# Moving 34 columns in place of 136 in the attention's products with the values

## The chip, the cores and the metric

The kernel runs on one core of a Trainium2 chip. The metric is the device time in microseconds (us) of one execution. Three executions of the kernel before took 1523.86, 1524.19 and 1518.64 us; the median is 1523.86 us. A fourth execution was profiled and took 1523.76 us.

## The reference

The input x has 4 sequences of 1024 tokens with 256 channels. Three layers follow one another, each on a layer norm of x and each added to x:

- a gated delta-rule attention with 16 heads of 16, whose state runs over the tokens in order;
- a cross attention on a context of 64 tokens;
- a feed-forward layer: a causal convolution, a pointwise product, a mixture of 8 experts of which 2 are taken, a norm and a small gelu network.

The change touches the cross attention alone. Cut to what matters it is:

```
q = (query @ Wq.T)   as 32 half heads of 8;  k likewise;  v = (value @ Wv.T) as 16 heads of 16
q1, q2 = q[:, :16], q[:, 16:];  k1, k2 = k[:, :16], k[:, 16:]
a1 = softmax(q1 k1^T * 8**-0.5) @ v
a2 = softmax(q2 k2^T * 8**-0.5) @ v
attn = a1 - lam * a2            # then a norm per head, and attn @ Wp.T + bp
```

## The kernel before, in words

The tokens are worked in 8 tiles (NI) of 4 sequences by 128 tokens. A tile has a first half (the recurrent attention, with its chunk steps z, d1, cs and co, its projections and the 16-token blocks "raw") and a second half (the cross attention and the feed-forward layer). The code is unrolled. Work of several tiles is interleaved: while the recurrence of one tile runs, the second half of the tile before it runs too, and the projections of the next tiles. The order of each engine is written out by hand in the lists ORDER["pe"], ORDER["dve"], ORDER["act"] and ORDER["pool"]; the engines meet through semaphores. The table KEEP says where TensorE issues products of the identity with itself, `keep` (line 1532), into a bank that nobody reads. They are left out wherever bank 7 is in use for good, which is most of the loop: the profile has none of them between 228 and 1222 us.

The cross attention of a tile runs in 8 units u. A unit is one sequence and 8 of its 16 heads:

- `sc` (line 1821) computes the scores of the 8 heads, 32 contraction rows at a time, into banks 4 and 5.
- VectorE takes the maxima (L1306) and subtracts them (L1312); ScalarE exponentiates (L786).
- `pt` (line 1841) transposes the probabilities, four heads per call, and ScalarE copies them to SBUF (L794).
- `pv` (line 1856) is the step that changes. For each of the 8 heads the transposed probabilities (128 by 128: two half heads with 64 context tokens each) are the stationary operand, and rows of vx_sb the moving one. A head owns 34 columns of vx_sb: for each half head 16 values and a column that gives the sum of the probabilities. The product of head h is written to the bank from column 34 h on.
- VectorE then takes the reciprocal of the sums (L1323) and forms a1 - lam * a2 (L1329, L1331, L1333).

Before the change each product of `pv` moves 136 columns, those of its own head and of the three that follow, and writes 136 columns of the bank. The columns behind its own 34 are overwritten by the products of the next heads, or are not read after the last. So that the last heads have something to read, vx_sb is 102 columns longer, and these are set to zero at the start (line 904).

All operands of these products are 4-byte floats. The profile shows every such product as two LDWEIGHTS and two MATMUL records. A unit has 8 products, so it is a block of 16 records of each kind; there are 8 units in each of 8 tiles: 64 blocks, 1024 records.

In the last tile the second half runs alone, and the units alternate between two sets of banks and buffers (`values_bank`, `probT_of`).

Of the kernel before, what the change touches and what calls it, by code (L numbers as in the profile page):

```python
# [25 lines left out]
P = 128  # L26
B, S, D = 4, 1024, 256
H, DH = 16, 16
NK = 64
NE, HID = 8, 64  # L30
# [8 lines left out]
NP_ = B * G * NC  # L39
# [40 lines left out]
class Chain:  # L80
# [16 lines left out]
    def do(self, ins):  # L97
        self.link(ins)
        self.wait()
# [86 lines left out]
def build(nc, x, out, weights, consts, cols, scratch, biases):  # L186
    ctx = ExitStack()
    with ctx:
        def sb(name, shape, dt=F32):
            return ctx.enter_context(nc.sbuf_tensor(name, shape, dt))  # L190
# [46 lines left out]
        ones3 = sb("ones3", [P, P], BF16)  # L237

        kbx = sb("kbx", [P, 2, B, 4 * NK])
        vx_sb = sb("vx_sb", [P, (B * H + 3) * 34])  # L240
# [6 lines left out]
        zc = sb("zc", [P, B])  # L247
        state = sb("state", [P, 4, G * B, DH])
        decayed = sb("decayed", [P, 4, G * B, DH])
        halo = sb("halo", [P, 6, B, 3])  # L250
        fT = sb("fT", [P, KC, B, TB + 2])
# [13 lines left out]
        vT = sb("vT", [P, NC, D])  # L265
# [10 lines left out]
        M3 = sb("M3", [P, NP_ + 1, CH])  # L276
# [30 lines left out]
        def values_bank(j):  # L307

            return bank[2 if j == NI - 1 else 6]
# [5 lines left out]
        def probT_of(j, u):  # L315
            flat_ = last_probT if j == NI - 1 and u % 2 else cs[:, 4, :]
            return flat_.rearrange("p (h t) -> p h t", h=8)
# [24 lines left out]
        gT = cs[:, 7, T:2 * T]  # L342
# [552 lines left out]
        def _(dve):  # L895
# [4 lines left out]
            do(V.memset(eps5, 1e-5))  # L900
            do(V.memset(eps6, 1e-6))
            do(V.memset(bias3[:, :], 0.0))
            for t_, value in ((ones3[:, :], 1.0), (zc[:, :], 0.0), (state[:, :, :, :], 0.0), (vT[:, :, :], 0.0), (M3[:, NP_:, :], 0.0), (vx_sb[:, B * H * 34:], 0.0), (fT[:, :, :, 0:2], 0.0), (halo[:, :, :, :], 0.0), (gT[HID:P, :], 0.0), (gT[HID:HID + 1, :], 1.0)):
                do(V.memset(t_, value))

            dve.wait_ge(ld_l, 16)
# [569 lines left out]
        def _(pe):  # L1476
            mm = nc.tensor.matmul
# [317 lines left out]
            def second(j):  # L1795
                def up(name, k=1):
                    pe.wait_ge(ev[name].sem, ev[name].at(j, k))

                def fin(name, ins):
                    ins.then_inc(ev[name].sem, 1)  # L1800
# [43 lines left out]
                def pv(u, n):  # L1844
                    b, hc = u // 2, u % 2
                    up("pt_sb", 2 * u + n + 1)
                    if n == 0:
                        if j == NI - 1:
                            if u:
                                up("a_sb", u)  # L1850
                        else:
                            up("pt_sb", 2 * u + 2)
                    for h in range(4 * n, 4 * n + 4):

                        at = (b * H + 8 * hc + h) * 34
                        last = mm(values_bank(j)[:, 34 * h:34 * h + 136], probT_of(j, u)[:, h, :], vx_sb[:, at:at + 136], start=True, stop=True)  # L1856
                    if n:
                        fin("pv_ps", last)

# [91 lines left out]
                def ffu_(p):  # L1951
                    up("gelu", p + 1)
                    for n in range(2):
                        b = 2 * p + n
                        last = mm(bank[TAIL[p]][:, D * n:D * n + D], gT[:, b * TB:b * TB + TB], ffu, start=True, stop=True)
                    fin("ffu_ps", last)

                return {"turn2": turn2, "qx": qx_, "sc": sc, "pt": pt, "pv": pv, "turn3": turn3, "wp": wp_, "turn4": turn4, "pw": pw_, "router": router, "moe": moe,
                        "turn5": turn5, "mi": mi, "mo": mo, "turn6": turn6, "ffd": ffd_, "ffu": ffu_}

# [86 lines left out]
```

## Time and profile before

| what | value |
|---|---|
| median of the three runs | 1523.86 us |
| time of the profiled execution | 1523.76 us |
| its span, first to last instruction | 1522.0 us |
| TensorE (PE) busy | 1433.8 us, 94% |
| weight loads (PEld) busy | 954.3 us, 63% |
| VectorE (DVE) busy | 1171.5 us, 77% |
| ScalarE (ACT) busy | 829.3 us, 54% |
| GpSimd (POOL) busy | 203.4 us, 13% |
| mean granted TensorE clock | 0.993 of 2.4 GHz |
| line 1856, MATMUL | 1024 records of 128 x 136 |

Busy is the time in which an engine has at least one instruction in flight; overlapping instructions are counted once. The mean duration of one MATMUL record is therefore longer than the distance between two of them. PEld is the loading of stationary operands, which overlaps the products. The granted clock is 1.00 at 2.4 GHz and 0.50 at 1.2 GHz; a stretch with a value between the two has been at both levels.

### The profile page before, as it was taken

What the parts mean: (1) busy time and instruction counts of PE and PEld (TensorE: products, weight loads), DVE (VectorE), ACT (ScalarE), POOL (GpSimd) and SP (SyncE); (2) the same over time, 40 slices, a digit from 0 to 9 for tenths busy, and PEclk for the clock granted to TensorE, in tenths of its full rate; (3) what the DMA queues carried; (4) which work ended last, traced back from release to release, by engine and by line L of the source; (5) the groups of instructions that cost most, each with busy time, mean ns of one, the idle gap of its engine ahead of it and who ended that gap; (6) DMA issues with size and microseconds to landing.
All of it is one profiled execution on the core that took longest, in us unless ns stands there. A gap on an engine that the chain in (4) does not pass through costs nothing.

```text
span 1522.0 us, 38260 instructions
## 1 busy us (share of the span) xinstructions
PE 1433.8 (94%) x15839; PEld 954.3 (63%) x15870; DVE 1171.5 (77%) x3193; ACT 829.3 (54%) x1596; POOL 203.4 (13%) x212
## 2 busy tenths in 40 slices
PE   3988999999999999999999999999999988999998
PEld 1654666755766566755766566755766567756765
DVE  7457878977897878977797878877797778855753
ACT  2555365646665565645665565645665564534443
POOL 0121111102200121102200122102200022101000
PEclk9999999999999999999999999999999999999999
DMA  5010001000100001100100001000100001000000
GB/s 234 1 29 30 2 22 15 24 1 15 29 29 2 2 29 16 30 2 15 29 29 2 2 21 23 31 1 16 29 15 2 2 29 24 8 1 15 1 1 14
DMA packets 20213, 31.28 MB, mean 21 GB/s; under 512 B 1480, under 2 KB 17864, under 8 KB 19784
## 3 DMA queue, kind: packets, MB, share of 16 engines
q1 hardware_dynamic: 20040, 28.82, 6.5%
q8 instruction: 127, 2.08, 0.6%
q14 instruction: 46, 0.38, 0.1%
HBM read 20.41 MB, written 8.39 MB: 19 GB/s over the span
## 4 chain that ended last, share of the span: by engine, by line
PE 79%; DVE 13%; ACT 5%; issue 2%; POOL 0%; DVEq 0%; ACTq 0%
PE bank L1913 15%; PE bank L1856 7%; PE bank L1482 6%; PE bank L1612 6%; PE four L1703 4%; PE bank L1821 4%; PE bank L1841 4%; PE bank L1507 4%; PE four L1771 3%; PE bank L1615 3%; PE bank L1532 3%; PE four L1755 2%; PE four L1507 2%; PE bank L1514 2%; PE four L1722 2%
## 5 line engine op out<-in xcount | busy, mean ns | idle before, releaser
L1913 PE MATMUL bank<-w_sb,cs 128*128 128x512 f32 x512 | 246.9, 600 | 1.5 <-ACT cs L840 0.3
L551 POOL TENSOR_TENSOR decayed<-state,pk 128x512 f32<-128x512 f32 x64 | 68.1, 1064 | 848.2 <-DVE state L1222 848.2
L840 ACT ACTIVATE cs<-bank 128x512 f32<-128x512 f32 x128 | 76.3, 596 | 182.8 <-PE bank L1488 85.9
L1913 PEld LDWEIGHTS bank<-w_sb,cs 128*128 128x128 f32 x512 | 94.3, 190 | 88.5 <-issue 81.3
L1430 DVE SCALAR_TENSOR_TENSOR cs<-cs,rwt 128x256 f32<-128x256 f32 x224 | 98.7, 487 | 42.1 <-ACT cs L840 42.1
L1856 PEld LDWEIGHTS bank<-vx_sb,cs 128*128 128x128 f32 x896 | 108.4, 189 | 27.4 <-ACT cs L794 18.0
L1856 PE MATMUL bank<-vx_sb,cs 128*128 128x136 f32 x896 | 119.3, 284 | 5.1 <-ACT cs L794 3.1
L1612 PE MATMUL bank<-hT,w_sb 128*128 128x512 f32 (+1 forms) x224 | 107.5, 602 | 3.0 <-ACT hid L662 1.4
L794 ACT COPY cs<-bank 128x512 f32<-128x512 f32 x116 | 67.5, 582 | 74.5 <-PE bank L1841 73.8
L1081 DVE SCALAR_TENSOR_TENSOR qkv<-pre,l_sb,qkv 128x512 f32<-128x512 f32 x144 | 100.4, 746 | 0.0
L786 ACT ACTIVATE cs<-cs 128x1024 f32<-128x1024 f32 x60 | 63.4, 1056 | 56.3 <-DVE cs L1312 55.8
L1306 DVE TENSOR_REDUCE pkc<-bank 128x8 f32<-128x512 f32 x120 | 77.6, 683 | 18.9 <-PE bank L1821 16.7
L1312 DVE TENSOR_TENSOR cs<-bank,pkc 128x512 f32<-128x512 f32 x120 | 77.0, 683 | 14.5 <-PE bank L1841 14.1
L1841 PE MATMUL bank<-c_sb,cs 128*128 128x128 f32 x464 | 74.1, 282 | 10.7 <-ACT cs L794 5.6
L586 ACT ACT_TABLE_LOAD x64 | 82.1, 1283 | 1.1
L1821 PE MATMUL bank<-kbx,cs 32*128 32x256 f32 x480 | 79.2, 400 | 1.4 <-ACT cs L781 1.4
L1482 PE MATMUL bank<-cs,w_sb 128*128 128x256 f32 (+1 forms) x320 | 79.8, 389 | 0.6 <-issue 0.2
L1205 DVE SCALAR_TENSOR_TENSOR shared<-four,c_sb 128x256 f32<-128x256 f32 x128 | 55.9, 478 | 23.8 <-PE four L1722 22.8
L1841 PEld LDWEIGHTS bank<-c_sb,cs 128*128 128x128 f32 x464 | 49.7, 140 | 36.5 <-issue 24.1
L1703 PEld LDWEIGHTS four<-kq,shared 64*64 64x64 f32 x2048 | 63.9, 135 | 13.3 <-issue 13.2
L1532 PEld LDWEIGHTS bank<-c_sb 128*128 128x128 f32 x550 | 68.0, 199 | 6.2 <-issue 5.4
L1703 PE MATMUL four<-kq,shared 64*64 64x48 f32 x2048 | 69.6, 220 | 2.2 <-POOL shared L533 1.1
(257 smaller groups left out, 2994.6 us busy)
## 6 DMA issues: line engine op xcount, KB each, us to landing
xt<-in_x SPq DMA_DIRECT2D x8, 512.0 KB, 4.9
vscr<-qkv SPq DMA_DIRECT2D x8, 512.0 KB, 2.7
vT<-vscr SPq DMA_DIRECT2D x32, 128.0 KB, 4.4
Tm<-in_x SPq DMA_DIRECT2D x8, 512.0 KB, 3.9
out<-cs SPq DMA_DIRECT2D x8, 512.0 KB, 2.9
w_sb<-in_weights SPq DMA_DIRECT2D x1, 3656.0 KB, 18.5
w_sb<-in_weights SPq DMA_DIRECT2D x1, 1456.0 KB, 8.5
cs<-in_scratch SPq DMA_DIRECT2D x3, 256.0 KB, 8.8
```

The lines of the kernel that those rows point to most:

```text
L586: nc.scalar.preload_act_table_set(name)
L1081: ins = stt(dst, pre[:, n % 4, :, t:TB + t], L("conv", 4 * n + t, 4 * n + t + 1), dst, ALU.mult, ALU.add)
L1430: ins = stt(comb[:, b, :], src, wgt, comb[:, b, :], ALU.mult, ALU.add)
L1482: last = mm(dst, lhs(k), rhs(k), start=k == 0, stop=k == n - 1)
L1507: last = mm(dst[:, D * n:D * n + D], lhs[:, k, b * TB:b * TB + TB], rhs[:, k, :], start=False, stop=n == 1 and k == 1)
L1532: mm(bank[7 if i > 0 else 6][:, 0:P], ident, ident, start=True, stop=True)
L1612: mm(dst, ctrl[:, k, at:at + n], hT[:, k, :], start=k == 0, stop=False)
L1703: last = mm(bank[RAW[c % 4]][q, 48 * n:48 * n + 48], kqb[q, c % 2, n, :], kq[q, g, b, c, :, :].rearrange("p x t -> p (x t)"), start=True, ...
L1821: last = mm(scores(j, u, a)[:, 256 * f:256 * f + 256], qx[r:r + 32, f, b * TB:b * TB + TB], kbx[r:r + 32, f, b, :], start=True, stop=True)
L1841: last = nc.tensor.transpose(turned_bank(j, n)[:, h * P:h * P + P], prob[:, 4 * n + h, :], ident)
L1856: last = mm(values_bank(j)[:, 34 * h:34 * h + 136], probT_of(j, u)[:, h, :], vx_sb[:, at:at + 136], start=True, stop=True)
L1913: mm(dst, x1T[:, k, b * TB:b * TB + TB], ew[:, k, ep * 512:ep * 512 + 512], start=k == 0, stop=False)
```

## The change

Each product of `pv` moves and writes the 34 columns of its own head. The zeroing of the 102 further columns of vx_sb is dropped, as nothing reads them any more. The buffer keeps its size; order, semaphores, banks and the KEEP table stay.

```diff
-            for t_, value in (... (M3[:, NP_:, :], 0.0), (vx_sb[:, B * H * 34:], 0.0), (fT[:, :, :, 0:2], 0.0), ...):
+            for t_, value in (... (M3[:, NP_:, :], 0.0), (fT[:, :, :, 0:2], 0.0), ...):
                 do(V.memset(t_, value))
...
                     for h in range(4 * n, 4 * n + 4):
                         at = (b * H + 8 * hc + h) * 34
-                        last = mm(values_bank(j)[:, 34 * h:34 * h + 136], probT_of(j, u)[:, h, :], vx_sb[:, at:at + 136], start=True, stop=True)
+                        last = mm(values_bank(j)[:, 34 * h:34 * h + 34], probT_of(j, u)[:, h, :], vx_sb[:, at:at + 34], start=True, stop=True)
```

## Rows read from the trace of the kernel before

**Rows 1.** The page: span; busy us, share, instructions; granted clock in 40 slices.

```profile
span 1522.0 us, 38260 instructions
PE 1433.8 (94%) x15839; PEld 954.3 (63%) x15870; DVE 1171.5 (77%) x3193; ACT 829.3 (54%) x1596; POOL 203.4 (13%) x212
PEclk9999999999999999999999999999999999999999
```

**Rows 2.** The page: the chain that ended last, by engine.

```profile
PE 79%; DVE 13%; ACT 5%; issue 2%; POOL 0%; DVEq 0%; ACTq 0%
```

**Rows 3.** Groups by line and shape: busy us, mean ns of one, idle before.

```profile
L1856 PE MATMUL bank<-vx_sb,cs 128*128 128x136 f32 x896 | 119.3, 284 | 5.1 <-ACT cs L794 3.1
...
L1897 PE MATMUL bank<-w_sb,cs 128*128 128x8 f32 x128 | 16.5, 252 | 1.3 <-DVE cs L1380 1.3
```

**Rows 4.** Windows, line 1856 alone: stretch, length, busy (records), clock, DMA.

```profile
228.00:1222.00 994.00, 102.27 (x768) 1.00 0.06 16
1222.00:1315.00 93.00, 17.06 (x128) 1.00 0.09 24
1394.00:1456.00 62.00, 16.86 (x128) 1.00 0.03 10
```

**Rows 5.** Timeline, one block of line 1856: start us, length us, what.

```profile
745.26 1.92 PEld L1856 LDWEIGHTS bank<-vx_sb,cs 128*128 128x128 f32 x16
745.26 2.12 PE L1856 MATMUL bank<-vx_sb,cs 128*128 128x136 f32 x16
...
747.31 0.74 PEld L1821 LDWEIGHTS bank<-kbx,cs 32*128 32x128 f32 x8
```

**Rows 6.** Timeline, weight loads of the 8-column products.

```profile
307.38 0.52 PEld L1897 LDWEIGHTS bank<-w_sb,cs 128*128 128x128 f32 x4
```

**Rows 7.** The chain in order of time, inside the loop.

```profile
977.58 1.12 PE bank L1856 x8
```

**Rows 8.** Windows, all engines: busy and records of each, clock, DMA.

```profile
1225.00:1230.00 5.00, 2.14 (x9) 1.01 (x7) 2.25 (x5) 4.34 (x7) 1.83 (x3) 1.00 0.00 0
...
1320.00:1325.00 5.00, 4.58 (x90) 4.06 (x90) 2.77 (x9) 0.62 (x2) 1.06 (x1) 0.66 0.01 3
...
1330.00:1335.00 5.00, 4.00 (x42) 3.14 (x41) 3.98 (x11) 2.46 (x4) 0.00 (x0) 0.96 0.00 0
1335.00:1340.00 5.00, 4.78 (x12) 2.92 (x13) 0.03 (x1) 1.22 (x3) 0.00 (x0) 0.70 0.00 0
```

**Rows 9.** Timeline of PE around the falls of the clock.

```profile
1320.42 0.45 PE L1755 MATMUL four<-rq,shared 32*64 32x64 f32 x14 [0.74 <-issue]
1320.81 1.55 PE L1532 MATMUL bank<-c_sb 128*128 128x128 f32 x6
...
1329.45 1.50 PE L1532 MATMUL bank<-c_sb 128*128 128x128 f32 x12
...
1331.31 0.46 PE L1755 MATMUL four<-rq,shared 32*64 32x64 f32 x16
1332.77 0.61 PE L1897 MATMUL bank<-w_sb,cs 128*128 128x8 f32 x4 [1.00 <-DVE cs L1380]
...
1339.17 1.88 PE L1913 MATMUL bank<-w_sb,cs 128*128 128x512 f32 x4
```

**Rows 10.** Timeline of PE, its longest idle stretch in the loop.

```profile
1229.94 2.43 PE L1507 MATMUL four<-w_sb,kn 128*128 128x256 f32 x10 [2.86 <-DVE kn L1254]
```

**Rows 11.** Timeline of PE: neighbours of a block, loop and last tile.

```profile
276.66 2.09 PE L1856 MATMUL bank<-vx_sb,cs 128*128 128x136 f32 x16
278.69 0.69 PE L1722 MATMUL four<-spare,M 64*32 64x128 f32 x32
...
1437.41 0.60 PE L1841 MATMUL four<-c_sb,mk 128*128 128x128 f32 x4
1439.01 2.12 PE L1856 MATMUL four<-vx_sb,mk 128*128 128x136 f32 x16 [0.99 <-ACT mk L794]
```

**Rows 12.** Timeline of DVE at the start: the memset that goes.

```profile
6.14 0.14 DVE L904 MEMSET vx_sb<- 128x102 f32 x1
```

More of the change, by code:

```diff
@@ L902, in _ @@
             do(V.memset(bias3[:, :], 0.0))
-            for t_, value in ((ones3[:, :], 1.0), (zc[:, :], 0.0), (state[:, :, :, :], 0.0), (vT[:, :, :], 0.0), (M3[:, NP_:, :], 0.0), (vx_sb[:, B * H * 34:], 0.0), (fT[:, :, :, 0:2], 0.0), (halo[:, :, :, :], 0.0), (gT[HID:P, :], 0.0), (gT[HID:HID + 1, :], 1.0)):
+            for t_, value in ((ones3[:, :], 1.0), (zc[:, :], 0.0), (state[:, :, :, :], 0.0), (vT[:, :, :], 0.0), (M3[:, NP_:, :], 0.0), (fT[:, :, :, 0:2], 0.0), (halo[:, :, :, :], 0.0), (gT[HID:P, :], 0.0), (gT[HID:HID + 1, :], 1.0)):
                 do(V.memset(t_, value))
```

## The prediction, made before the changed kernel ran

> **What bounds the kernel now.** I read the page first. TensorE is busy 94% of the span and no other engine is above 77% [rows 1]; the chain that ended last lies on TensorE for 79% [rows 2]. The granted clock is above nine tenths in all 40 slices, so TensorE almost always runs at 2.4 GHz. In the list of groups the products of line 1856 are the second largest: 119.3 us for the 896 records outside the last tile, 133 ns of busy time each [rows 3]. The windows show where they lie: 768 records (48 blocks of 16) in the loop, 128 at its end, 128 in the last tile, all at full clock [rows 4]. Inside the loop the chain in order of time runs through such blocks [rows 7], so their length counts.
>
> **What a block costs, and what the narrower product saves.** From the timeline of one block [rows 5]: 16 weight loads take 1.92 us; one load alone is 0.19 us in this view (186 to 190 ns), so two starts are (1.92 - 0.19) / 15 = 115 ns apart. What sets the 115 ns? The products of 512 columns give the price of a column: four take 1.88 us and one of them 0.60 (such a group's mean), so (1.88 - 0.60) / 3 = 0.43 us for 512 columns, 0.84 ns each [rows 9]. 136 columns need 114 ns. The present block is bound by the columns, but barely. The nearest row for a narrow moving operand behind a full 128 x 128 weight load is the router's, with 8 columns [rows 6]: four loads in 0.52 us, (0.52 - 0.19) / 3 = 110 ns apart. With 8 columns to move (7 ns) only the load can be setting this. So a product of 34 columns (28 ns) is not four times faster; its block becomes bound by the weight loads at 110 ns. I take the router's pace.
>
> - Pace: 16 x (115 - 110) = 0.08 us per block.
> - Tail: where the next step uses another shape of rows, as `sc` with 32 rows does, it starts only when the last product has drained, 747.31 - 745.26 = 2.05 us after the block's start [rows 5]. The last product is shorter by 102 x 0.84 = 0.09 us, of which I count 0.08. By the written order some 44 of the 64 blocks have such a successor (`sc`, z, cs, co); the others are followed by 128-row work.
> - Sum: 64 x 0.08 + 44 x 0.08 = 8.6 us of TensorE's time. Bounds: 0, if what follows waits for another engine anyway, and 9 us, if all of it is on the chain. That is the whole direct gain: 0.6% of the time, though 102 of 136 columns go.
> - The memset on VectorE lasted 0.14 us at 6.14 us [rows 12]. It lies beside the first loads, ahead of any product. I count nothing; 0.2 us with its gap is the most.
> - VectorE's reciprocal waits for the block, and gets it 0.16 us earlier. That is the same gain, not a second one. No wait, transfer or instruction is added.
>
> **What the columns did besides.** The clock fell in only a few places, and the rows show what TensorE did ahead of them [rows 8, 9]. Between 1330 and 1335 us it worked on little: 16 products of 64 columns that run four abreast (0.46 us), 1.00 us of idling, and then the router's 8-column products, 0.61 us for the first four, in which the array moves columns for 4 x 7 = 28 ns. PEld was busy 3.14 of these 5 us. Then the clock fell: 1335 to 1340 shows 0.70. The stretch up to 1320.8 is alike, with narrow products four abreast and an idle 0.74 us; 1320 to 1325 shows 0.66. So weight loads did not hold the clock up, and "busy" records with few columns did not either. On the other side stands an idle stretch of 2.86 us ahead of 1229.94, with 512- and 256-column products before and behind it, and its 5 us show 1.00 [rows 8, 10].
>
> A present block moves columns for 16 x 114 ns = 1.8 of its 2.05 us. After the change it is 16 x 28 ns = 0.45 of 1.9 us: much like the router's stretch, but longer. A loop without filler products has 48 such blocks, and the steps beside them are often narrow too [rows 11]: 32 products of 128 columns in 64-row groups right behind one block, and in the last tile four transposes and 0.99 us of idling ahead of another. I therefore expect the clock to fall to 1.2 GHz behind a part of the blocks.
>
> What a fall costs: 5 x (1 - 0.66) = 1.7 us of full-speed work in the one case, 5 x (0.04 + 0.30) = 1.7 in the other [rows 8]. That it takes real time off TensorE is shown by the filler products: 12 in 1.50 us at full clock, 6 in 1.55 us behind the fall [rows 9]. With the chain on TensorE for 79%, and some of the rest released by it, I take 85%: 1.45 us per fall in the loop. Bounds 0 and 1.7. At the end of the loop and in the last tile other engines hold the pace more often (0.99 us of waiting for ScalarE's copy ahead of one block [rows 11]), and I take 0.8.
>
> How many: between 0 and 64, one per block. No row shows a block with 34 columns, so this is the soft term. Laying out the columns moved in each stretch of the trace with 28 ns in place of 114, and comparing with what stood ahead of the falls seen, I find one loop block in three as thin as those (16 of 48), and 9 of the last 16, which stand among waits.
>
> Sum: 1523.8 - 8.6 + 16 x 1.45 + 9 x 0.8 = 1523.8 - 8.6 + 23.2 + 7.2 = 1545.6. I take 1545. This stands on the profiled execution, 1523.76 us, of which 1.76 lie outside its span; the median of the runs is 1523.86, so nothing has to be shifted.
>
> The Trainium skill speaks against this part. Its page "TensorE: Matmul & The Clock Gate", in the table of the section "Why this matters for your kernels", warns of long idle gaps between bursts of matmuls as what drops the clock in mid-kernel. The change makes no gap longer, so by that rule nothing falls, and the sum would be 1523.8 - 8.6 = 1515.2. The trace does not side with it: the 2.86 us gap kept the clock and thin stretches with gaps of 1.00 and 0.74 us lost it.
>
> **The rivals.**
>
> - A: the clock holds. The blocks get shorter, nothing else happens: 1515, faster. For it: the loop's clock is 1.00 over 994 us, with narrow steps in it too, and PEld would be nearly full inside a block. Against it: the router's stretch in rows 9 had full weight loads too. 0.15.
> - B: falls and gain cancel, with some 2 to 10 falls, or the clock holds and the gain is swallowed by waits: 1517 to 1531. For it: rows 8 hold the only two falls behind the loop and rows 4 show none in its 994 us, so the margin may be wide there. 0.13.
> - C: the fall comes behind almost every block: 48 x 1.7 + 16 x 1.0 = 98 us on 1515, 1613; with half of the blocks at these prices it is 1564. For it: 64 blocks all lose the same columns. Against it: most have 256- or 512-column products close by. Beyond 1580 I give 0.08.
> - D: the columns alone set the pace, and the weight loads hide. Then a block would shrink by 16 x (115 - 28) = 1.4 us, 64 of them by 89 us: 1435. The router's 110 ns at 8 columns speaks plainly against it. 0.02.
>
> **How the numbers follow.** My forecast, falls behind a quarter to two thirds of the blocks, has 0.62; its own range is 1531 to 1580. About 0.5% (7.6 us) is what a measurement of this kernel can tell from no change. Slower by more than that is the forecast and C: 0.70. Within it is B: 0.13. Faster is A, whose 8.6 us only just pass the bound, and D: 0.17. The range for 8 in 10 has to reach towards A and stops ahead of the worst of C: 1514 to 1580.
>
> **What would show it.** In the changed profile the block's 16 weight loads should take 15 x 0.110 + 0.19 = 1.84 us and the next step start about 1.89 us after its beginning. If loads are 115 ns apart as before, or 40 ns, the pace step is wrong. The windows of the loop should show granted clocks of 0.6 to 0.8 in some 5 us stretches with line 1856, where now all are 1.00, and the mean clock should drop from 0.993 to about 0.965 (25 falls x 1.7 us in 1545). Products in these stretches should be twice as far apart. If the mean clock stays at 0.99 or above, the main term is wrong and A holds; if falls are as many as forecast but the time is not, the price of 1.45 us is wrong, because TensorE has slack there.

## The result

The kernel with 34 columns takes 1611.7 us (median of 6 runs, 1606.29 to 1615.88) against 1523.49 (median of 6, 1518.64 to 1526.43). The ratio is 1.058, with a 95% interval of 1.0555 to 1.0604: 88 us slower. The direction of the forecast was right, the size was not: 1545 was predicted, with 1580 as the upper end.

The page of the changed kernel (span; busy time of the engines; granted clock in 40 slices; the chain by engine), to be held against [rows 1, 2]:

```profile
span 1614.1 us, 38290 instructions
PE 1536.8 (95%) x15870; PEld 1034.7 (64%) x15870; DVE 1175.2 (73%) x3192; ACT 829.7 (51%) x1596; POOL 203.5 (13%) x212
PEclk9999998899789998899889998899879996799699
PE 84%; DVE 10%; ACT 4%; issue 2%; POOL 0%; DVEq 0%; ACTq 0%
```

VectorE, ScalarE and GpSimd are busy as long as before, within 4 us. TensorE is busy 103 us longer, with the same instructions but for the narrower products (31 matmul records are missing from the trace of before), and its clock, which was above nine tenths in every slice, is below in 15 of the 40. The row of all cores gives the mean clock:

```profile
core 0: 1614.1 us, clock 0.916
```

As the clock has two levels, 2.4 and 1.2 GHz, the time at the lower one is 2 x (1 - 0.916) x 1614.1 = 271 us, against 2 x (1 - 0.993) x 1522.0 = 21 us before. The six runs of the changed kernel show the same relation among themselves: 1615.88 us at a mean clock of 0.916 and 1606.29 at 0.922. The kernel before shows it too: over the 53 runs of it that were timed beside the experiments (mean clocks from 0.990 to 0.996), a fitted line gives 0.41 us of time per us at the low clock.

Where the low clock lies, in windows of line 1856 alone (columns as in [rows 4], with PEld's busy time after PE's; the stretches are the loop, its end and the last tile):

```profile
228.00:1305.00 1077.00, 113.06 (x768) 108.17 (x768) 0.92 0.06 15
1305.00:1398.00 93.00, 19.99 (x128) 19.04 (x128) 0.75 0.07 19
1488.00:1560.00 72.00, 23.96 (x128) 23.12 (x128) 0.74 0.00 1
```

The same stretches of the kernel before showed 1.00 [rows 4].

**A block at the full clock** does what was predicted. Weight loads of one in the loop, and the start of the step behind it, in the timeline:

```profile
274.46 1.86 PEld L1856 LDWEIGHTS bank<-vx_sb,cs 128*128 128x128 f32 x16 [0.38 <-ACT cs L794]
276.36 0.18 PEld L1821 LDWEIGHTS bank<-kbx,cs 32*128 32x128 f32 x1
```

(1.86 - 0.19) / 15 = 111 ns from load to load, where 110 were predicted and 115 stood before [rows 5]; the next step starts 1.90 us after the block's beginning, where 1.89 were predicted and 2.05 stood before.

**A block at the low clock**, behind such a fall, one tile later:

```profile
462.66 0.70 PE L1755 MATMUL four<-rq,shared 32*64 32x64 f32 x16
463.30 1.11 PE L1841 MATMUL bank<-c_sb,cs 128*128 128x128 f32 x4
464.34 0.70 PE L1755 MATMUL four<-rq,shared 32*64 32x64 f32 x16
465.18 1.09 PE L1841 MATMUL bank<-c_sb,cs 128*128 128x128 f32 x4
466.19 1.13 PE L1722 MATMUL four<-kn,M 64*32 64x128 f32 x32
467.26 3.63 PE L1856 MATMUL bank<-vx_sb,cs 128*128 128x34 f32 x16
470.81 1.13 PE L1722 MATMUL four<-spare,M 64*32 64x128 f32 x32
471.67 0.90 PE L1739 MATMUL four<-state,kq 64*32 64x64 f32 x32
472.50 1.11 PE L1514 MATMUL bank<-c_sb,cs 128*128 128x128 f32 x4
...
475.76 0.66 PE L1841 MATMUL bank<-c_sb,cs 128*128 128x128 f32 x4
```

Four transposes take 1.11 us here and 0.66 once the clock is back; 32 products of 128 columns 1.13 in place of 0.69 [rows 11]. The block takes 3.63 us, although it moves few columns, because the weight loads slow down with the array:

```profile
467.25 3.49 PEld L1856 LDWEIGHTS bank<-vx_sb,cs 128*128 128x128 f32 x16 [0.38 <-ACT cs L794]
```

One such load lasts 0.33 us (the median in the last tile, at the low clock), so they start (3.49 - 0.33) / 15 = 211 ns apart. TensorE hardly waits between 460.6 and 476 us. It is busy all the time, mostly with steps that move few columns, and the low clock lasts: the trace's record of the clock has it from 461.3 to 475.0 us.

### The profile page after: what moved, and what is told of

Same layout as the page of the kernel before. It is cut to its first block, busy times and chain, and to the rows that moved or that the text cites. A ratio compares the mean times of both kernels' runs of the same rounds, so it can differ in the third digit from the quotient of the medians.

```text
span 1614.1 us, 38290 instructions
## 1 busy us (share of the span) xinstructions
PE 1536.8 (95%) x15870; PEld 1034.7 (64%) x15870; DVE 1175.2 (73%) x3192; ACT 829.7 (51%) x1596; POOL 203.5 (13%) x212
## 3 DMA queue, kind: packets, MB, share of 16 engines
q8 instruction: 127, 2.08, 0.5%
## 4 chain that ended last, share of the span: by engine, by line
PE 84%; DVE 10%; ACT 4%; issue 2%; POOL 0%; DVEq 0%; ACTq 0%
PE bank L1913 14%; PE bank L1856 7%; PE bank L1612 6%; PE bank L1482 6%; PE bank L1841 5%; PE bank L1821 4%; PE four L1703 4%; PE bank L1507 4%; PE bank L1532 3%; PE bank L1615 3%; PE four L1771 3%; PE four L1722 3%; PE four L1755 3%; PE bank L1514 2%; PE four L1507 2%
## 5 line engine op out<-in xcount | busy, mean ns | idle before, releaser
L1856 PEld LDWEIGHTS bank<-vx_sb,cs 128*128 128x128 f32 x896 | 127.2, 225 | 31.3 <-issue 15.4
L1856 PE MATMUL bank<-vx_sb,cs 128*128 128x34 f32 x896 | 133.1, 309 | 4.1 <-ACT cs L794 3.1
L1612 PE MATMUL bank<-hT,w_sb 128*128 128x512 f32 (+1 forms) x224 | 119.5, 660 | 3.0 <-ACT hid L662 1.4
L1841 PE MATMUL bank<-c_sb,cs 128*128 128x128 f32 x464 | 93.1, 335 | 7.0 <-DVE cs L1333 3.8
L1821 PE MATMUL bank<-kbx,cs 32*128 32x256 f32 x480 | 89.4, 440 | 1.4 <-ACT cs L781 1.4
L1841 PEld LDWEIGHTS bank<-c_sb,cs 128*128 128x128 f32 x464 | 63.6, 169 | 35.6 <-issue 26.8
L1703 PEld LDWEIGHTS four<-kq,shared 64*64 64x64 f32 x2048 | 69.5, 145 | 13.8 <-issue 13.7
L1532 PEld LDWEIGHTS bank<-c_sb 128*128 128x128 f32 x550 | 73.4, 212 | 7.0 <-issue 6.2
L1703 PE MATMUL four<-kq,shared 64*64 64x48 f32 x2048 | 75.5, 230 | 2.2 <-POOL shared L533 1.1
```

What stands on the lines that cost most here:

```text
L1532: mm(bank[7 if i > 0 else 6][:, 0:P], ident, ident, start=True, stop=True)
L1612: mm(dst, ctrl[:, k, at:at + n], hT[:, k, :], start=k == 0, stop=False)
L1703: last = mm(bank[RAW[c % 4]][q, 48 * n:48 * n + 48], kqb[q, c % 2, n, :], kq[q, g, b, c, :, :].rearrange("p x t -> p (x t)"), start=True, ...
L1821: last = mm(scores(j, u, a)[:, 256 * f:256 * f + 256], qx[r:r + 32, f, b * TB:b * TB + TB], kbx[r:r + 32, f, b, :], start=True, stop=True)
L1841: last = nc.tensor.transpose(turned_bank(j, n)[:, h * P:h * P + P], prob[:, 4 * n + h, :], ident)
L1856: last = mm(values_bank(j)[:, 34 * h:34 * h + 34], probT_of(j, u)[:, h, :], vx_sb[:, at:at + 34], start=True, stop=True)
```

## The experiments

Each is the kernel before with the width of line 1856 (1857 in the variants) changed. The memset of the 102 further columns stays in all of them, so a loss that they show isn't due to its absence. The diffs show the width.

**Width: 68, 102 and 128 columns.**

```diff
-  ... vx_sb[:, at:at + 136] ...
+  ... vx_sb[:, at:at + wide] ...      # wide = 68, 102, 128; the bank's columns likewise
```

> Each product of line 1856 moves 68 columns (its own head and the next). Theory 1, the clock is lost for want of moved columns: a product moves columns for 57 of its 110 ns instead of 28, so part of the falls goes and the rest is shorter; about 1545 us, between 1525 and 1590, mean clock 0.95 to 0.985. Theory 2, the loss comes with leaving 136 at all (the overlap of the written columns, the order of the products) and not with their number: as with 34, 1612 us and 0.916.

> Each product of line 1856 moves 102 columns. Theory 1: 86 ns of columns in 110 ns keep the clock nearly as 136 do; 1515 to 1530 us, clock 0.985 or more. Theory 2 (any width under 136 costs the same): 1612 us.

> Each product of line 1856 moves 128 columns: 107 ns of columns, just under the 110 ns of a weight load. The clock keeps by both the columns and the order; the blocks go at the pace of the weight loads, so 64 x 0.08 = 5 us less than before: 1518 us. If the pace of 115 ns before was not set by the columns, no change: 1523.

Measured, each ratio against the runs of the kernel before that were timed beside it (medians 1522.2 us for 68, 102 and 128 columns, 1523.5 for 34, 1523.1 for 170), and together with the other widths. The mean clock is that of all runs of the row, and the low-clock time is 2 x (1 - clock) x span in their mean:

| columns | median us | ratio, 95% interval | mean clock | us at the low clock |
|---|---|---|---|---|
| 34 (the change) | 1611.7 | 1.0579 [1.0555, 1.0604] | 0.919 | 261 |
| 68 | 1531.3 | 1.0078 [1.0038, 1.0119] | 0.980 | 61 |
| 102 | 1523.7 | 1.0005 [0.9987, 1.0024] | 0.989 | 33 |
| 128 | 1522.0 | 0.9995 [0.9982, 1.0009] | 0.991 | 26 |
| 136 (before) | 1522.2 | | 0.994 | 19 |
| 170 | 1548.0 | 1.0164 [1.0145, 1.0184] | 0.994 | 18 |

The loss goes with the number of columns and not with leaving 136: theory 2 is out. Half of the columns (68) already avoid nine tenths of the loss. The 68-column kernel is the uneasy one: its six runs spread from 1524.92 us (mean clock 0.987) to 1543.67 (0.970). With 128 the expected 5 us did not show in the median, and the clock accounts for most of them. The ten runs are 26 us at the low clock and the 21 beside them 19, and at 0.40 those 7 or 8 us cost 3. At equal mean clock the gain is there: 1518.20 and 1518.23 us at 0.993, where four runs of before took 1522.37 to 1524.36. Over the clocks that both kernels reached (0.992 to 0.994) it is 3.3 to 5.4 us. So 128 columns give the direct gain, and a little of the clock goes even there.

**170 columns.**

> 170 columns per product, so the columns set the pace: 142 ns in place of 115 per record. 1024 x 28 ns = 29 us more, at a clock of 0.993 or more: 1548 us if blocks are on the chain throughout, at least 1540. If moved columns beyond 136 still removed falls, a few us less.

The buffer vx_sb is one head (34 columns) longer here. 1548.0 us, 25 us over before; 29 were expected from the columns alone (the 1548 that was named is less than before plus 29, which is 1552). Sixteen weight loads take 2.32 us, so they start (2.32 - 0.19) / 15 = 142 ns apart, as the price of a column had it. So the columns set the pace from 136 up, and the blocks are on the chain nearly throughout. At 68, 102 and 128 columns the sixteen loads take 1.86 us, as with 34: there the weight loads set it. That confirms the first step of the prediction from its other side.

**34 and 136 in turn.**

```diff
+  wide = 136 if u % 2 else 34
```

> 34 columns in the even units, 136 in the odd ones. Theory 1a, every thin block costs by itself: half of the 88 us, 1567. Theory 1b, the low clock keeps itself up because thin blocks follow one another, above all in the last tile: falls are ended sooner, clearly under half of the loss, 1535 to 1550, and the 37 us stretch at the low clock in the last tile is gone.

1564.9 us (1554.58 to 1574.29), ratio 1.030 [1.023, 1.036]: 43 us lost, half of 88, as theory 1a has it. But the 37 us stretch at the low clock in the last tile is gone, which was 1b's sign: the windows from the first to the last block of that tile (length, PE busy, clock) are

before, after, and in turn:

```profile
1415.99:1449.28 33.29, 30.79 (x232) 1.00 0.01 1
```

```profile
1494.75:1541.40 46.65, 46.63 (x231) 0.60 0.00 1
```

```profile
1447.21:1482.65 35.44, 33.18 (x232) 0.90 0.00 1
```

So the sum alone misled; each theory kept one of its two signs. The last pair of experiments tests whether all blocks cost the same.

**34 columns in the last tile alone.**

```diff
+  wide = 34 if j == NI - 1 else 136
```

> 34 columns in the 8 blocks of the last tile alone, 136 in the other 56. The two traces put 13.5 us of the whole 88 between the first and the last block of that tile (the changed kernel is 78.8 us behind at its first block and 92.1 at its last, less what comes back at the end). If the loss is local to the thin blocks: 1522 + 12 = 1534 us, between 1528 and 1540. If the low clock there was inherited from the loop's falls before it: 1522 to 1526.

1532.8 us, ratio 1.0065 [1.0048, 1.0082]: 9.7 us for 8 blocks. The window is as long as with 34 everywhere (46.65 us), with no thin block ahead of it:

```profile
1412.02:1458.64 46.62, 46.60 (x231) 0.60 0.00 1
```

The loss is local; nothing is inherited from the loop. The window is 13.3 us longer than before, for 37.5 us at the low clock. The profiled run lost only 9.4 us in all, as it came to the tile 4 us early: the two short falls of before, at 1320.9 and 1334.6 us, are absent from it.

**More work, less time.**

```diff
+  wide = 34
...
+  if h % 4 == 0:
+      mm(values_bank(j)[:, 272:512], probT_of(j, u)[:, h, :], vx_sb[:, 0:240], start=True, stop=True)
```

> 34 columns as in the changed kernel, and in each call of four products one further product of 240 columns into the unused columns 272 to 511 of the same bank, read by nobody. It is pure extra work: two records of some 0.20 us per call, 0.8 us per block, 51 us in all at the full clock. Theory 1 (the loss is the clock, and moved columns hold it): the clock comes back to 0.985 or more, and the time is 1522 - 8 + 51 = 1565 us, 45 us FASTER than the changed kernel with less work. Theory 2 (the loss is something else in the narrow products): 1612 + 51 = 1663 us.

1569.4 us (1568.02 to 1570.72), mean clock 0.989: 42 us faster than the changed kernel, with 128 further products that nobody reads. Theory 2 had 1663. The filler in the loop, in a window of its line alone:

```profile
228.00:1305.00 1077.00, 64.92 (x196) 30.25 (x196) 0.99 0.06 16
```

The whole stretch is at 0.99 again, where the change had 0.92. This is the plainest proof that the loss is the clock, and that added products, which move columns, hold it. That it is their columns, and not just more busy time, rests on the widths above: there the number of products stays.

**What makes a fall long: one wide block, or a burst, in the last tile.** Both start from the kernel with 34 columns in the last tile alone.

```diff
+  wide = 34 if j == NI - 1 and u != 4 else 136        # the first
+  KEEP = {(NI, -1, "sc", 5, 0): 24, ...               # the second, widths as in the last tile alone
```

> As the kernel with 34 columns in the last tile alone (1532.8 us, one fall of 37.5 us there), but its unit 4 moves 136 columns again; the other seven keep 34. What makes a fall long is the question. Theory 1, at the low clock the same steps move half as many columns in a given time, so the clock stays down until a step with many columns comes: the 37.5 us stretch ends or is broken about at unit 4 and time comes back, 1528 to 1531 us, half-clock time in the last tile 15 to 30 us. Theory 2, a fall is as long as the attention's loop whatever it moves: 37.5 us and 1532.8 again.

> As the kernel with 34 columns in the last tile alone, and after its unit 4 24 filler products of 128 columns (48 records, 5.3 us at the full clock), read by nobody. Theory 1: the clock comes back within these fillers and the stretch of 37.5 us ends there, perhaps with a new fall behind; half-clock time in the tile about 25 us, and of the 5 to 8 us of extra work some 2 to 4 come back: 1535 to 1538 us. Theory 2 (nothing thin or wide matters once it is down): 37.5 us or more, and 48 x 0.21 = 10 us on top, 1543.

1534.1 us (1526.12 to 1542.0) and 1535.4 us (1530.82 to 1544.81). The first missed the 1528 to 1531 of theory 1 and lies at or above theory 2's 1532.8; the second lies where theory 1 had it. Neither decides it. Both profiled runs are among the fastest of their kernels, and in them the clock held through the first five and six blocks of the tile, where it had fallen ahead of the third before. The long fall wasn't there to end; a fall of 10.2 us came further on, at 1440.4 and 1445.1 us. In the second the fillers also stood one block earlier than I wrote, behind unit 3. The two longest runs of the first kernel (1542 us) have a mean clock of 0.979, 64 us at the low clock, so one wide block doesn't keep long falls away in every run. Where the tile loses the clock differs from run to run.

**A wide block just ahead of a regular fall, and one inside it.** In the loop the changed kernel falls at the same places of five of its six tiles, so these are better targets.

```diff
+  wide = 136 if u == 5 else 34        # the first
+  wide = 136 if u == 6 else 34        # the second
```

> 34 columns as in the changed kernel, but unit 5 of each tile moves 136 again. In the changed kernel's trace the longest regular falls (13.7 us, in tiles 0, 1, 2, 3 and 5, and 17.1 us in tile 4) begin just behind unit 5's block, at 277.0 us in tile 0. Theory L (a fall is called by what was moved just before it): these falls go or begin later, behind unit 6, and are shorter; per tile up to 13.7 us of low clock less, worth 0.4 of it: 6 x 5 = 30 us, 1582 us. Theory E (each block has an equal share of the 88 us): 8 blocks of 64 give 11 us, 1601.

> 34 columns as in the changed kernel, but unit 6 of each tile moves 136 again. Unit 6's block lies inside those falls (283.2 to 286.7 us in tile 0, in a fall from 277.0 to 290.7). Theory L: the falls begin at the same place, and end 3 to 7 us sooner because the block inside them moves four times the columns at the low clock at the same pace of 0.22 us per record; 6 x 5 x 0.4 = 12 to 15 us, 1597. If a fall once begun isn't shortened by a wider block: 1605 to 1611. Equal shares: 1601, so the length of the falls in the trace has to tell.

Measured: 1573.7 us (ratio 1.032 [1.027, 1.037]) and 1594.9 us (1.048 [1.041, 1.054]). One block of eight made wide again gives back 38 us of 88 in the one place and 17 in the other; equal shares would be 11. By the intervals, the first is well above an equal share (31 to 47 us); the second (6 to 25) isn't clear of it. The windows from the start of unit 5 to that of unit 7 in tile 1, in order: before, changed, unit 5 wide, unit 6 wide:

```profile
442.44:458.46 16.02, 15.35 (x325) 1.00 0.01 2
```

```profile
458.70:479.83 21.13, 20.91 (x326) 0.68 0.01 2
```

```profile
455.07:470.94 15.87, 15.20 (x325) 1.00 0.01 2
```

```profile
453.14:473.06 19.92, 19.70 (x325) 0.74 0.01 2
```

With unit 5 wide the fall behind it isn't there, in this and in the five other tiles: 1.00, and 15.87 us, even less than before, as unit 6 is still narrow. With unit 6 wide the fall begins where it did, and ends 0.5 us behind the wide block, at 466.1 us. The timeline of that kernel:

```profile
453.14 1.95 PE L1857 MATMUL bank<-vx_sb,cs 128*128 128x34 f32 x16
455.01 2.13 PE L1821 MATMUL bank<-kbx,cs 32*128 32x256 f32 x8
...
460.60 1.13 PE L1722 MATMUL four<-kn,M 64*32 64x128 f32 x32
461.67 3.99 PE L1857 MATMUL bank<-vx_sb,cs 128*128 128x136 f32 x16
465.59 0.87 PE L1722 MATMUL four<-spare,M 64*32 64x128 f32 x32
466.27 0.66 PE L1739 MATMUL four<-state,kq 64*32 64x64 f32 x32
466.85 0.66 PE L1514 MATMUL bank<-c_sb,cs 128*128 128x128 f32 x4
```

The four transposes of L1514 behind the block take 0.66 us here and 1.11 at the same place of the changed kernel. In the last tile of the kernel with unit 5 wide the long fall ends in the same way:

```profile
1488.20 3.96 PE L1857 MATMUL four<-vx_sb,mk 128*128 128x136 f32 x16
1492.10 1.14 PE L1821 MATMUL four<-kbx,cs 32*128 32x256 f32 x8
```

L1821 took 2.08 us ahead of that block and 1.14 behind it. So in these places a fall is called by the few columns moved just ahead of it, and a wide block inside it cuts it short.

A general law for the length of a fall isn't shown, and two places in tile 1 speak against a simple one. The changed kernel's own fall ended at 475.0 us with no wide product ahead of it, behind eight transposes of 128 columns and in a narrow step; the next wide products start at 476.74. With unit 6 wide the same tile lost the clock again behind unit 7, from 476.3 to 490.0 us, and two records of 512 columns at 477.23 didn't end that fall. The whole tile (first block to first block) was even slower there than in the changed kernel:

```profile
404.31:592.93 188.62, 185.52 (x1912) 0.89 0.06 15
```

```profile
409.91:594.08 184.17, 181.29 (x1916) 0.92 0.06 16
```

Over the six tiles the falls at the place of unit 6 add up to 41 us where the changed kernel has 86. At 0.40 that is worth 18 us, against the 17 measured; tile 1 shows that such a gain can come back as another fall.

**128 columns, 34 for the last product.**

```diff
+  wide = 34 if h == 7 else 128
```

> 128 columns for seven products of a block, 34 for the last one, whose drain the next step waits for. Clock as before. If the shorter tail counts on the chain: 0.06 + 0.08 us per block, 6 to 8 us under before, 1515. If it is swallowed by what follows, as the 128 columns alone showed (1522.0 against 1522.2): 1521.

1518.4 us (1515.86 to 1521.15) beside 1523.1 of before, ratio 0.9969 [0.9956, 0.9982]: 4.7 us faster than the kernel before, and 93 faster than the change. Its block in the timeline:

```profile
743.56 1.86 PEld L1857 LDWEIGHTS bank<-vx_sb,cs 128*128 128x128 f32 x16
745.46 0.52 PEld L1821 LDWEIGHTS bank<-kbx,cs 32*128 32x128 f32 x6
```

It has the 1.90 us of the narrow block and keeps the columns of seven products. At equal mean clock (0.991 to 0.994) it is 5.5 to 7.4 us faster than the runs beside it; the median shows less, as its runs are 27 us at the low clock and those beside them 21. This is the version to use; the change as made isn't.

## Why the prediction was wrong

- **Pace and tail of a block: right.** 111 ns and 1.90 us against 110 and 1.89. Rival D (the columns alone set the pace) is refuted, by these loads and by 170 columns costing 25 us.
- **The gain of 8.6 us: not measured by itself,** since no kernel with 34 columns kept its clock. 128 columns with the short tail have the same block length and gained 4.7 us, and 5.5 to 7.4 at equal mean clock, so most of it was real.
- **That the clock falls behind thin blocks: right.** It was read from two stretches of the trace [rows 8, 9], and the widths and the filler show it. Rival A is refuted, and so is the rule that only idle gaps matter: the changed kernel waits less at the place shown, and falls. One half of my argument against that rule was weak: a gap of 2.86 us that kept the clock doesn't say that longer gaps do. The trace of before has one of 3.63 us, ahead of 31.49 us, in which the clock fell.
- **How many falls: near, in part by luck.** 25 were counted on, 16 in the loop and 9 behind it. The record of the granted clock shows 16 in the loop where there were none, and 6 between it and the last block where there were 2: 20 more. Whether the 16 stand behind the blocks that I had in mind isn't on record.
- **What a fall costs: this is the step that failed.** I took 1.7 us of full-speed work, and so 1.45 us of time, from two falls of before [rows 8]. The step took it for granted that a new fall would be as short as those. Measured it is (88 + 9) / 20 = 4.9 us. The price of a us at the low clock was about right: 97 us for the 261 - 19 = 242 more, or 0.40, where 1.45 out of 2 x 1.7 had assumed 0.43. What was wrong is the length: these 22 falls last 3.4 to 37.5 us, 11.6 in the mean, and not 3.4. The trace of before already had a fall twice as long in thin work, which I left out of the sum, ahead of the first block:

```profile
170.00:175.00 5.00, 4.36 (x104) 3.74 (x105) 4.86 (x12) 0.00 (x0) 1.06 (x1) 0.56 0.01 3
175.00:180.00 5.00, 5.00 (x36) 5.00 (x36) 4.90 (x14) 1.60 (x3) 0.00 (x0) 0.75 0.00 0
```

  That is 5 x (0.44 + 0.25) = 3.5 us of full-speed work, with TensorE busy for 9.36 of the 10 us. I had looked at what stood ahead of the falls, and not at what ended them. In the one from 1334.6 to 1338.0 us the router's stretch is followed at once by products of 512 columns:

```profile
1333.74 2.94 PE L1913 MATMUL bank<-w_sb,cs 128*128 128x512 f32 x4
```

  In the loop a thin block is followed by transposes and narrow steps, and the clock stays down through them. The two experiments with a wide unit fit this; but the other short fall, at 1320.9 us, had no wide product in it [rows 9], so why the old falls were short is shown only in part. At the low clock, moreover, each step takes twice as long for the same columns, and this applies to the weight loads too (211 ns), so a thin stretch also becomes a long one.
- **The last tile** was to cost 9 x 0.8 = 7 us with the blocks just before it. Alone, its 8 blocks cost 9.7, in one long fall and not in several. The window from its first to its last block grew by 13.3 us for 37.5 us at the low clock, 0.36 per us and so near the 0.40 of the whole, though TensorE had waited for 2.5 of its 33.29 us before.
- **The range:** rival C's 1613 is nearly the measured time, but by another sum: almost 64 short falls, where 20 long ones came. Its nearness is luck. It was given 0.08 beyond 1580. The range stopped short because it took the number of falls as the only soft term, and held their length fixed.

## What to carry to other kernels

Where the weight loads set the pace of small products, columns up to that pace cost next to nothing (128 here), and they hold the clock; taking them away as waste cost 5.8%. Trim only what a successor waits for, here the last product of a block. When a change makes TensorE's work thinner, ask two things of every stretch: what was moved just ahead, and how far off the next wide step is. Here the length of the falls, and not their number, made the price.

## What the runs showed of the hardware that I had not expected

- The low clock slows the weight loads as it does the products: 111 ns from load to load at the full clock, 211 behind a fall. The narrow block takes 3.55 us to the next step there (467.26 to 470.81) and the wide one 3.92 (461.67 to 465.59, unit 6 wide), so narrow products save 0.37 us per block at the low clock, and the low clock costs the narrow block 1.65.
- A PE that is busy all the time can stay at the low clock for long. In the last tile the window of 46.65 us has 46.63 us busy and a mean clock of 0.60.
- Adding 128 products made the kernel 42 us faster. And where only part of the work is thin, one and the same kernel spreads over more from run to run: 19 us in six runs with 68 columns, 20 in four with 34 and 136 in turn, 20 in four with unit 6 wide, against 10 in the six runs of the change and 8 in six of the kernel before.
